# One hidden-layer product moved ahead of the first output tiles, and the last store split over two queues

## The reference

```
xn  = layernorm(x)
s   = causal_attention(xn @ WQ, xn @ WK, xn @ WV)          # scores / sqrt(256)
r   = sum over the token's 2 picked experts of
      (silu(w*xn @ w1[e]) * (w*xn @ w3[e])) @ w2[e]        # added to token rows 0..7, see below
sh  = (silu(xn @ sw1.T) * (xn @ sw3.T)) @ sw2.T            # the shared network
out = x + s * silu(sh + r)
```

## Time and profile before

| | |
|---|---|
| Median of 3 runs | 235.4 us (235.35 to 235.5) |
| The profiled execution's own time | 234.9 us |
| Its span in the trace | 232.8 us |
| TensorE busy (matmuls) | 223.8 us, 96% |
| VectorE busy | 183.6 us, 79% |
| ScalarE busy | 150.3 us, 65% |
| GpSimd busy | 67.0 us, 29% |
| TensorE clock granted | full in all 40 slices |

### The profile page before, as it was taken

The page is one execution under the profiler, slowest core; times in us unless marked ns, Lnnn a source line. Parts: engine busy times, 40 slices in busy tenths (PEclk is TensorE's granted clock), DMA queues, the critical chain, the costliest instruction groups (busy, mean ns, idle before and its releaser), DMA issues.

```text
span 232.8 us, 4647 instructions
## 1 busy us (share of the span) xinstructions
PE 223.8 (96%) x1500; PEld 199.8 (86%) x1500; DVE 183.6 (79%) x618; ACT 150.3 (65%) x403; POOL 67.0 (29%) x120
## 2 busy tenths in 40 slices
PE   6899999999999999999999999899999999999983
PEld 5788899998998998989989988798888989889743
DVE  3878659799798898897699897778686776769765
ACT  2454755856856747658557674697869686788712
POOL 5321732853656538529020200002020120202000
PEclk9999999999999999999999999999999999999999
DMA  5699520020200200001000000129754638384322
GB/s 173 205 326 303 171 93 1 5 88 8 73 17 8 90 4 6 1 8 34 0 3 1 0 4 0 48 32 220 201 84 147 122 103 183 74 197 71 112 86 96
DMA packets 19319, 19.78 MB, mean 85 GB/s; under 512 B 1176, under 2 KB 18272, under 8 KB 19296
## 3 DMA queue, kind: packets, MB, share of 16 engines
q1 hardware_dynamic: 16128, 16.35, 23.2%
q0 software_dynamic: 3168, 3.15, 9.1%
HBM read 15.15 MB, written 4.34 MB: 84 GB/s over the span
## 4 chain that ended last, share of the span: by engine, by line
PE 91%; DVE 3%; ACT 2%; DMA 2%; issue 1%; SPq 1%; DVEq 0%; ACTq 0%
PE bank L440 83%; PE bank L535 4%; PE bank L489 3%; DMA raw_qkv<-in_L_attn_WK 2%; ACT arena L779 1%; DVE raw_sw L1476 1%; DVE w L1474 1%; DVE arena L1016 1%; PE bank L623 1%; ACT w L945 0%; PE bank L462 0%; DVE arena L1401 0%; SPq L233 0%; ACT xT_hi_all L779 0%; ACT probs L779 0%
## 5 line engine op out<-in xcount | busy, mean ns | idle before, releaser
L440 PE MATMUL bank<-xT_hi_all,arena 128*128 128x512 f32 (+3 forms) x256 | 78.8, 365 | 0.7 <-DVE arena L1016 0.7
L440 PE MATMUL bank<-arena 128*128 128x256 f32 (+1 forms) x496 | 69.3, 285 | 0.8 <-DVE arena L1016 0.7
L440 PEld LDWEIGHTS bank<-arena 128*128 128x128 f32 (+1 forms) x496 | 62.8, 182 | 5.5 <-DVE arena L1016 1.8
L440 PEld LDWEIGHTS bank<-xT_hi_all,arena 128*128 128x128 f32 x256 | 46.8, 188 | 6.9 <-DVE arena L1016 0.9
L779 ACT ACTIVATE arena<-bank 128x512 fp32r<-128x512 f32 (+4 forms) x83 | 36.0, 455 | 24.7 <-PE bank L440 23.3
L1016 DVE TENSOR_TENSOR arena<-bank,arena 128x264 fp32r<-128x264 f32 (+4 forms) x83 | 41.5, 509 | 12.7 <-ACT arena L779 12.4
L440 PE MATMUL bank<-xT_lo_all,arena 128*128 128x512 f32 (+3 forms) x128 | 45.9, 358 | 0.0
L431 POOL DMA_DIRECT2D x_ring<-in_L_attn_x x6 | 7.9, 1316 | 71.3 <-DVE x_ring L1411 71.3
L440 PEld LDWEIGHTS bank<-xT_lo_all,arena 128*128 128x128 f32 x128 | 24.2, 189 | 2.2
L809 ACT ACTIVATE probs<-bank,neg_max 128x128 f32<-128x128 f32 (+3 forms) x32 | 17.0, 531 | 13.0 <-DVE neg_max L1074 12.9
L1401 DVE SCALAR_TENSOR_TENSOR arena<-w,w_rows,arena 128x128 fp32r<-128x128 f32 x64 | 18.2, 346 | 6.7 <-ACT arena L779 6.7
(11 more groups left out here) (132 smaller groups left out, 398.1 us busy)
## 6 DMA issues: line engine op xcount, KB each, us to landing
x_ring<-in_L_attn_x SPq DMA_DIRECT2D x7, 512.0 KB, 3.5
x_ring<-in_L_attn_x POOLq DMA_DIRECT2D x6, 512.0 KB, 5.9
out<-x_ring SPq DMA_DIRECT2D x6, 512.0 KB, 3.3
spread<-pairs SPq DMA_DIRECT2D x14, 128.0 KB, 3.6
w_sb<-in_L_ffn_w SPq DMA_DIRECT2D x1, 1024.0 KB, 11.2
raw_sw<-in_L_ffn_sw SPq DMA_DIRECT2D x3, 256.0 KB, 4.4
x_ring<-in_L_attn_x SPq DMA_DIRECT2D x2, 256.0 KB, 3.0
xn<-in_L_attn_x SPq DMA_DIRECT2D x1, 512.0 KB, 6.5
```

The source lines that it names most:

```text
L440: return nc.tensor.matmul(dst, lhsT, rhs, start=start, stop=stop, skip_group_check=True, **kw)
```

## The change

Two edits that don't touch each other.

1. On TensorE, `hidden(1, 1, 1)` (the fourth product of the second batch's shared network) is written behind `gather(0, 1)`, ahead of the loop, and left out of `step2(1)`.
2. The store of the last token tile takes rows 0 to 63 from SyncE's queue and rows 64 to 127 from ScalarE's queue. ScalarE issues no other transfer. The final wait counts five completions instead of four.

```diff
@@ SyncE
             for t in range(T):
                 sp.wait_ge(s["last_summed"], t + 1)
-                sp.dma_start(out_v[0, :, t:t + 1, :], x_last[:, t:t + 1, :]).then_inc(s["last_stored"], 16)
+                rows = slice(0, P if t < T - 1 else P // 2)
+                sp.dma_start(out_v[0, rows, t:t + 1, :], x_last[rows, t:t + 1, :]).then_inc(s["last_stored"], 16)
...
-            sp.wait_ge(s["last_stored"], 16 * T)
+            sp.wait_ge(s["last_stored"], 16 * (T + 1))
@@ TensorE
             hidden(1, 1, 0, h1_bank, "h1_done")
             gather(0, 1)
+            hidden(1, 1, 1, h3_bank, "h3_done")
             pe.wait_ge(s["pairs_kept"], 1)
...
                 gather(i, 1)
-                hidden(i, 1, 1, h3_bank, "h3_done")
+                if i > 1:
+                    hidden(i, 1, 1, h3_bank, "h3_done")
                 accumulate(i - 1, 1)
@@ ScalarE
                 nc.scalar.activation(gate[:, t, :], src[:, 0:D], ACT.Silu).then_inc(s["last_gate_done"], 1)
+            act.wait_ge(s["last_summed"], T)
+            act.dma_start(out_v[0, P // 2:P, T - 1:T, :], x_last[P // 2:P, T - 1:T, :]).then_inc(s["last_stored"], 16)
```

## The result

| | before | changed |
|---|---|---|
| Median | 235.4 us (5 runs, 235.18 to 235.5) | 236.73 us (5 runs, 236.09 to 237.06) |
| Ratio | | 1.0057, 95% interval 1.0045 to 1.0069 |
| Profiled execution, its span | 234.9 us, 232.8 us | 236.09 us, 234.0 us |

The change makes the kernel 1.3 us slower. The forecast was 0.3 us slower, with a range that ended at 236.3.

The account below looks back on a forecast made before the run. TensorE's chain was taken as the bound, with a ScalarE and VectorE path meeting it at `shared_out(1, 0)`. Terms +0.42 (edit 1) and -0.10 (edit 2) gave +0.32, so 235.4 + 0.3 = 235.7 us; eight-in-ten range 235.1 to 236.3.

Parts of the forecast that it names:

- The two paths that meet at `shared_out(1, 0)`: At 160.6 us, TensorE's own work (ready 160.53) and a path over ScalarE and VectorE (`h_low(1, 1)` ending 160.57) meet.
- (a): After `gather(0, 1)`, the product and a 0.12 us clearing matmul start `shared_out(0, 0)` at 151.72 instead of 151.21, 0.5 us back.
- (b): A group following work takes 1.90 us to its gather, after a pause 1.99; `gather(1, 0)` starts at 153.62, 0.42 us late.
- my upper bound, 0.60: The delay of `shared_out(1, 0)` if clearing bank 7 costs 0.30 us instead of 0.12.
- (c): On ScalarE, `silu_rows(1, 0)` waits for the gather and starts 0.42 us late; VectorE's `h_low(1, 1)` then ends at 160.99.
- (e): Later batches, rounds of 10.29 us without a pause in TensorE's matmuls, carry the whole 0.42 us to the end.
- (d): TensorE's stream ends at 159.10, then waits 1.9 us for `h_lo`; `shared_out(1, 0)` starts at 161.04, +0.42 us.
- -0.1 us: The split last store's term, taken nearer to 0 than to the 0.25 us gain, since the engines are shared.
- The straight line through 256 and 128 KB to 64 KB: Store landings of 2.2 and 1.7 us give 1.45 for 64 KB: a 0.25 us gain if the halves share nothing.
- ScalarE's first transfer is slow: Rival at the last store: first use of ScalarE's queue costs up to 0.8 us, time 236.2 or 236.6; chance 0.18.
- The filled pause: Rival: TensorE's 0.67 us pause before the first output tiles is filled, nothing else moves, time 234.6; chance 0.12.
- The clock rival: Rival: TensorE's new 1.9 us pause costs clock, matmul rounds at half clock costing microseconds; chance 0.02.

Follow-up runs that it names:

- half product: Three of the moved product's six matmuls ahead of the output tiles, three at the old place, against the kernel before: ratio 1.0001.
- gather ahead: Moved product, store whole, and in batch 1 `gather(1, 0)` ahead of `accumulate(0, 0)`, against the kernel before: ratio 1.0014.

## Why the prediction was wrong

- **What bounds the kernel: right.** The two paths that meet at `shared_out(1, 0)`, and the one over `gather(1, 0)`, ScalarE and VectorE as the one that edit 1 lengthens, are what the runs show: from `gather(0, 1)` to `shared_out(1, 0)` it is 10.87, 10.87, 11.15 and 11.56 us where `gather(1, 0)` is 0, 0, 0.24 and 0.70 us late (before, half product, gather ahead, edit 1). This part gave the right direction.
- **Edit 1, (a) and (b): the mechanism right, the size too small.** The shift of `shared_out(1, 0)` was put at 0.42 us and measured 0.69 (11.56 - 10.87). From `gather(0, 1)` to `gather(1, 0)` I had 3.87 us; it took 4.15. The parts: the clearing matmul started 1.92 us behind the gather, not 1.85; it held the tiles back 0.23 us, not 0.12; and the sixteen matmuls to the gather took 2.00 us, not 1.90. The last was my step (b), that a group behind work is 0.1 shorter than one behind a pause. It doesn't hold here: the group takes 2.00 us in the half-product run as well, where there is no pause, and in the kernel before it takes 1.89 or 1.90 from 171.01 us on, where it follows a `hidden` product without a wait. Even my upper bound, 0.60, was passed.
- **Edit 1, (c) to (e): right.** From `gather(1, 0)` to `shared_out(1, 0)` it takes 7.41 us (7.42 before), and none of the shift was given back in the later rounds. In (d) TensorE's own stream ended at 159.53 (159.30 + 0.23), not 159.10, so the pause was 1.60 us where 1.9 was forecast; this changes nothing in the time, since the other path sets it. The wait is at L1021, not L1019.
- **Edit 2: the step that failed.** "I take -0.1 us", between a gain of 0.25 and nothing, measured +0.56 in the tail. The straight line through 256 and 128 KB to 64 KB gave 1.45 us from issue to landing; a half of 64 rows lands after 2.0 to 2.2 us. The line took bytes for what sets the landing. Where 64 KB keep all 128 rows they do land 0.1 us sooner than a whole tile on SyncE (1.6), far less than the line's 0.25, and not at all sooner on ScalarE (1.8). The reason I gave for a small term, that 64-row halves still use all the engines, had no row of such a store behind it. And the loss wasn't, as the rival had it, the first use of ScalarE's queue: it stays when the queue has been used, and grows when ScalarE takes no part. The rival "ScalarE's first transfer is slow" had the place and nearly the size (0.4), for the wrong reason. Of the 0.56 us, 0.5 are the later landing of ScalarE's half (2.2 against 1.7 us, from the start of the issue), and 0.22 of these are its longer issue (0.556 against 0.338). The rest lies between the end of the issue and the landing. That 64 rows are slow is shown; why they are is open.
- **The rule from the Trainium skill** ("DMA: Bandwidth & Descriptors", "Issuing engines are not separate DMA queues"), by which the edit would be worth 0, came nearer than my -0.1: no run here gains anything from the second queue. The runs show a loss in place of the 0, of 0.56 us in the tail.
- **The rivals.** The filled pause gave nothing, as the half product shows most clearly; it needed `h_low(1, 1)` to end by 159.9, and that ended at 161.24. The clock rival is out: the clock stays at 1.00 over the pause.

Sum of the steps: forecast +0.42 - 0.10; measured +0.69 + 0.56 = +1.25, against 1.2 between the profiled spans and 1.3 between the medians. Of the miss of 0.93 us, 0.66 are the store's term and 0.27 the delay's. With the store's term alone at its measured size the forecast would have been 235.4 + 0.42 + 0.56 = 236.4, outside the range; with the delay's alone 236.0, inside. So the right direction came from edit 1, and the store's term, forecast as a gain, is the step that broke the number.

## What to carry to other kernels

Where an engine pauses, work moved into the pause is free only up to the pause's length; every instruction of the moved work that sticks out delays what stands behind it, so look at who waits for that before at how much is moved. When two paths meet within hundredths of a microsecond, measure a change of either against both: each alone gave nothing or a loss here, together 1.1 us. Nothing hides a last store: before splitting it, look for a row of exactly that shape, since its size said little here.

## What the runs showed of the hardware

- A store of 64 rows of 1 KB was issued in 0.51 us from SyncE and 0.55 to 0.56 from ScalarE (0.59 as the second of two on SyncE), one of 128 rows in 0.34 and 0.38, whether the rows carried 1 KB or 512 bytes; 96 rows took 0.345 (SyncE) and 32 rows 0.406 (ScalarE), in one execution each. Landing, from the start of the issue: 2.0 us from SyncE and 2.2 from ScalarE for 64 rows; 1.7 and 1.8 for 128 rows of 1 KB, 1.6 and 1.8 for 128 rows of 512 bytes; 1.8 for the 96 rows, 2.0 for the 32.
- An issue by ScalarE 5 us before the end changed nothing: 0.546 us for its half against 0.556 where the queue was new.
- A pause of 1.6 us in TensorE's stream left the granted clock at 1.00. In the kept traces it fell only after the last matmul, if at all (0.50 from 232.0 to 233.0 us in the half product's).
